# Smaller tiles for the in-chunk inverse of a gated delta rule: 32-token tiles on TensorE, two reductions moved off VectorE, and a new order

## What is computed

```python
q = l2norm(x @ Wq); k = l2norm(x @ Wk); v = x @ Wv      # per head
q, k, v = (silu(causal_conv4(t)) for t in (q, k, v))
beta = sigmoid(x @ Wb)
g = -exp(A_log) * softplus((x @ Wfa) @ Wfb + dt_bias)   # decay per channel
def step(S, (q, k, v, g, b)):                           # over the tokens
    S = S * exp(g)[..., :, None]
    err = v - einsum('bhk,bhkv->bhv', k, S)
    S = S + b * k[..., :, None] * err[..., None, :]
    return S, einsum('bhk,bhkv->bhv', q, S)
out = rmsnorm(attn) * rms_scale * sigmoid((x @ Wga) @ Wgb)
x = x + out @ Wo
```

## Time and profile before

| | |
|---|---|
| median of 3 runs | 1009.48 us (1007.05 to 1011.78) |
| the profiled execution, its own time | 1013.73 us |
| its span, first to last instruction | 1011.9 us |
| mean granted TensorE clock | 0.982 |
| TensorE busy | 949.9 us, 94% |
| VectorE busy | 812.7 us, 80% |
| ScalarE busy | 708.2 us, 70% |
| GpSimd busy | 73.9 us, 7% |

### The profile page before, as it was taken

How to read it: one execution, slowest core, us unless ns; L and a number is a source line. 1 busy time by engine, 2 the same in 40 slices (tenths; PEclk the granted TensorE clock), 3 DMA queues, 4 the chain that set the end, 5 groups by cost and what they waited for, 6 DMA issues and landing times.

```text
span 1011.9 us, 34566 instructions
## 1 busy us (share of the span) xinstructions
PE 949.9 (94%) x15274; PEld 721.6 (71%) x15274; DVE 812.7 (80%) x1707; ACT 708.2 (70%) x1556; POOL 73.9 (7%) x179
## 2 busy tenths in 40 slices
PE   4888699999999999999999999999999998999986
PEld 3534367777777777777777777777777777788774
DVE  5577679889888888889888898888888888777644
ACT  2376658887787778787778787877877787545441
POOL 7000000000000000000000000000000000000010
PEclk9898789999999999999999999999999999999999
DMA  6100010100000101200001000200000000000001
GB/s 164 49 1 13 29 31 31 41 13 13 13 3 2 31 31 31 72 13 13 13 2 29 21 17 28 82 13 3 13 13 13 13 13 13 13 13 3 3 2 42
DMA packets 29033, 24.14 MB, mean 24 GB/s; under 512 B 4626, under 2 KB 24276, under 8 KB 28884
## 3 DMA queue, kind: packets, MB, share of 16 engines
q1 hardware_dynamic: 28884, 21.94, 7.9%
HBM read 20.82 MB, written 1.11 MB: 22 GB/s over the span
## 4 chain that ended last, share of the span: by engine, by line
PE 87%; DVE 5%; ACT 4%; POOL 2%; issue 1%; POOLq 0%; DVEq 0%; ACTq 0%
PE psum L824 17%; PE psum L847 10%; PE psum L888 8%; PE psum L870 8%; PE psum L879 7%; PE psum L947 6%; PE psum L834 3%; PE psum L925 3%; PE psum L830 3%; PE psum L919 3%; PE psum L912 3%; PE psum L905 3%; PE psum L839 2%; PE psum L854 2%; PE psum L898 2%; PE psum L936 2%
## 5 line engine op out<-in xcount | busy, mean ns | idle before, releaser
L824 PE MATMUL psum<-hT,gw 128*128 128x512 f32 x384 | 189.9, 621 | 1.7 <-DVE pairs L1275 0.9
L847 PEld LDWEIGHTS psum<-kq,ks 128*64 128x64 f32 x3072 | 106.3, 139 | 74.8 <-issue 44.0
L1231 DVE SCALAR_TENSOR_TENSOR qkv<-pad,chan,qkv 128x512 f32<-128x512 f32 x192 | 135.7, 754 | 0.3
L847 PE MATMUL psum<-kq,ks 128*64 128x64 f32 x3072 | 124.0, 227 | 8.8 <-DVE tot L1269 4.5
L1257 DVE TENSOR_TENSOR kq<-kq,tot 128x512 f32<-128x512 f32 x160 | 110.3, 689 | 25.0 <-PE psum L847 25.0
L824 PEld LDWEIGHTS psum<-hT,gw 128*128 128x128 f32 x384 | 69.1, 197 | 64.3 <-issue 61.0
L1275 DVE COPY_PREDICATED pairs<-masks,psum 128x256 f32<-128x256 uint8 x192 | 102.1, 532 | 4.1 <-PE psum L847 4.1
L870 PE MATMUL psum<-tmat,pairs 64*64 64x32 f32 x2560 | 102.3, 220 | 2.9 <-ACT tmat L556 2.5
L870 PEld LDWEIGHTS psum<-tmat,pairs 64*64 64x64 f32 x2560 | 89.5, 135 | 18.9 <-issue 11.5
L888 PE MATMUL psum<-pairs,fmat 64*64 64x32 f32 x2560 | 101.8, 220 | 0.9 <-DVE fmat L1242 0.9
L888 PEld LDWEIGHTS psum<-pairs,fmat 64*64 64x64 f32 x2560 | 90.0, 136 | 9.1 <-issue 5.8
(11 more groups left out here) (163 smaller groups left out, 1695.0 us busy)
## 6 DMA issues: line engine op xcount, KB each, us to landing
bb<-beta_rows SPq DMA_DIRECT2D x32, 256.0 KB, 3.3
gw<-in_L_attn_Wq SPq DMA_DIRECT2D x16, 128.0 KB, 2.2
gw<-in_L_attn_Wk SPq DMA_DIRECT2D x16, 128.0 KB, 2.3
gw<-in_L_attn_Wv SPq DMA_DIRECT2D x16, 128.0 KB, 2.2
gwo<-in_L_attn_Wo SPq DMA_DIRECT2D x4, 512.0 KB, 5.8
x<-in_L_attn_hidden_states SPq DMA_DIRECT2D x4, 256.0 KB, 4.4
gfb<-in_L_attn_Wfb SPq DMA_DIRECT2D x16, 64.0 KB, 2.1
ggb<-in_L_attn_Wgb SPq DMA_DIRECT2D x4, 256.0 KB, 4.9
```

The costliest lines, as they stand in the source:

```text
L824: last = eng.matmul(two(bank[to]), gw[:, t, kt, hh * D:(hh + 1) * D], two(hT[:, kt])[:, :, h * PW:(h + 1) * PW], start=(kt == 0), stop=(kt ...
L847: last = eng.matmul(o[rows(b), :, u], ks[:, p, tokens(b, u)], half(kq[:, p, :, tokens(b, u)], h, 1), start=True, stop=True)
L1231: last = eng.scalar_tensor_tensor(out=piece(t, i), in0=src, scalar=tap_weight(t, tap, i), in1=piece(t, i), op0=ALU.mult, op1=ALU.add)
```

## The change

Four things are done at once.

1. **Tiles of 32 tokens.** Levels 0 to 4 never join a token of the first 32 of a cell with one of the last 32. So `level_products` (levels 0 to 4), `first_natural`, `inverse_y`, `inverse_natural` and `inverse_turned` (levels 1 to 4) issue, for each cell, two products of half the size on the diagonal blocks instead of one: 16 products (32 records), each with 32 stationary columns and a moving side half as wide. `inverse_y` and `inverse_turned` of level 5 keep 64 columns and contract over 32 tokens instead of 64. `diagonal` and level 5's products stay as they are. Since the off-diagonal blocks are no longer written, the banks are zeroed once at the start, and GpSimd clears a block of `tt` in each step.
2. **Output squares.** ScalarE squares in four instructions of 128x128 with `accum_out`, which give the sums; VectorE's `tensor_reduce` of 128x512 goes.
3. **Decay totals.** `tots[1]` (128x256) and `tots[2]` (128x128) are formed on GpSimd instead of VectorE.
4. **Order.** Every engine's `slot` is written in another order, with other PSUM banks and other waits. The silu of the keys and queries, the first decay and level 0 of a step stand one slot earlier on ScalarE and VectorE.

```diff
+QUARTER = P // 4
-L_BANK = (2, 0, 2, 0, 1, 0)
-Y_BANK = (None, 1, 3, 3, 3, 3)
+L_BANK = (7, 3, 0, 0, 6, 1)
+Y_BANK = (None, 3, 4, 1, 5, 4)
...
+        def block_of(ap, b, u, j):
+
+            return ap[quarter(b, j), u * C + j * QUARTER:u * C + (j + 1) * QUARTER]
...
+            def block_totals(p, l, first=None):
+                if l:
+                    lower, upper = totals(l)
+                    return eng.tensor_tensor(tots[l + 1], lower, upper, ALU.mult)
+                lower, upper = first_pairs(first)
+                return eng.tensor_tensor(tots[1].rearrange("p (m n) -> p m n", m=G * B), lower, upper, ALU.mult)
+
+            def clear_turned(p):
+                for b in range(B):
+                    last = eng.memset(tt[quarter(b, 1), p, :].rearrange("p (u i) -> p u i", i=C)[:, :, 0:QUARTER], 0.0)
+                return last
...
+            def square_output():
+                for u in range(G):
+                    last = eng.activation(unit(osq, u), unit(bank[O_BANK], u), ACT.Square, accum_out=ssq[:, 0, u:u + 1])
+                return last
...
-                    eng.activation(osq, bank[O_BANK][:, :], ACT.Square).then_inc(osq_ready, 1)
...
             def level_products(p, l):
                 h = LEVELS[l]
                 o = bank[L_BANK[l]][:, 0:UC].rearrange("p (a u n t) -> p a u n t", a=2, u=G, t=h)
+                if l == NL - 1:
+                    for u in range(G):
...
+                per = QUARTER // (2 * h)
                 for u in range(G):
                     for b in range(B):
-                        last = eng.matmul(o[rows(b), :, u], ks[:, p, tokens(b, u)],
-                                          half(kq[:, p, :, tokens(b, u)], h, 1), start=True, stop=True)
+                        for j in range(2):
+                            at = slice(u * P + b * C + j * QUARTER, u * P + b * C + (j + 1) * QUARTER)
+                            to = slice(b * C + j * QUARTER, b * C + (j + 1) * QUARTER)
+                            last = eng.matmul(o[to, :, u, j * per:(j + 1) * per], ks[:, p, at],
+                                              half(kq[:, p, :, at], h, 1), start=True, stop=True)
                 return last
...
+            def block_products(o, l, left, right, upper):
+                h = LEVELS[l]
+                per = QUARTER // (2 * h)
+                for u in range(G):
+                    for b in range(B):
+                        for j in range(2):
+                            last = eng.matmul(o[quarter(b, j), u, j * per:(j + 1) * per], block_of(left, b, u, j),
+                                              half(block_of(right, b, u, j), h, upper), start=True, stop=True)
+                return last
...
-                        last = eng.matmul(o[rows(b), u], cell(nmat[:, l], b, u), half(cell(tmat, b, u), h, 0),
-                                          start=True, stop=True)
+                        last = eng.matmul(o[rows(b), u], cell(nmat[:, l], b, u)[0:QUARTER], half(cell(tmat, b, u), h, 0)[0:QUARTER],
+                                          start=True, stop=True)
...
+            eng.memset(psum[:, :, 0:UC], 0.0)
...
-                eng.tensor_tensor(ks_l, ks_l, upper, ALU.mult)
-                return eng.tensor_tensor(tots[1].rearrange("p (m n) -> p m n", m=gb), lower, upper, ALU.mult)
+                return eng.tensor_tensor(ks_l, ks_l, upper, ALU.mult)
...
-                    eng.tensor_reduce(ssq[:, 0], gd(osq), AX.X, ALU.add).then_inc(ssq_ready, 1)
```

More of the change, by code:

```diff
@@ L876, in inverse_natural @@
                 o = bank[TM_BANK[l]][:, 0:HC].rearrange("p (u n t) -> p u n t", u=G, t=h)
-                for u in range(G):
-                    for b in range(B):
-                        last = eng.matmul(o[rows(b), u], cell(tt[:, p], b, u), half(cell(fmat[:, l - 1], b, u), h, 0),
-                                          start=True, stop=True)
-                return last
+                return block_products(o, l, tt[:, p], fmat[:, l - 1], 0)
             def inverse_turned(p, l):
@@ L1254, in decays @@
                 if l:
-                    lower, upper = (tots[l].rearrange("p (n t) -> p n t", t=2)[:, :, i] for i in range(2))
+                    lower, upper = totals(l)
                     nb = HU // h
@@ new lines, in slot @@
+                if 0 <= nm1 < NCK:
+                    after(kraw_ready, nm1 + 1)
+                    eng.wait_ge(in_beta[q], 16 * (nm1 // 2) + 16)
+                    eng.tensor_tensor(ks[:, q], kraw[:, 0], bb[:, q], ALU.mult).then_inc(kb_ready, 1)
+                if 0 <= n0 < NCK:
+                    after(level4_done, n0 + 1)
+                    decays(p, 4)
+                    after(y3_done, n0 + 1)
+                    inverse_sum(3).then_inc(summed3, 1)
+                    keep_pairs(p, 4).then_inc(kept4, 1)
@@ new lines, in slot @@
+                if 0 <= nm1 < NCK:
+                    after(level0_done, nm1 + 1)
+                    decays(q, 0, chunk(dec, nm1 % NCH))
+                if 0 <= n1 < NCK:
+                    after(osq_ready, n1 + 1)
+                    eng.scalar_tensor_tensor(out=og, in0=gate[:, n1 % 2], scalar=1.0, in1=bank[O_BANK][:, :], op0=ALU.add, op1=ALU.mult).then_inc(og_ready, 1)
+                if 0 <= nm1 < NCK:
+                    after(diag_ready, nm1 + 1)
+                    keep_pairs(q, 0).then_inc(kept0, 1)
@@ L1396, in _ @@
             ln_centre(2, 0)
-            for t in range(NCK - 2, NCK + 1):
+            for t in range(NCK - 2, NCK):
                 slot(t)
             ln_scale(2, 0)
+            slot(NCK)
+            ln_move(2, 0)
             slot(NCK + 1)
```

638 lines of the change are left out of this document (341 added, 297 removed).

## The result

The changed kernel takes **983.1 us** (median of 4 runs, 976.8 to 987.7) where the kernel before took 1010.6 beside it on the same chip. The ratio is 0.972, with an interval of 0.969 to 0.976: 2.8% faster, where 7.8% were forecast. The direction and the range hold, the likeliest value is 52 us too low. Medians here count every execution; the ratios leave out those over 1.5% above the fastest of the same kernel. The profiled execution of the changed kernel is the fastest of its four, 976.8 us.

A forecast was written before the change was run, and what follows sets the result against it. TensorE was taken to bound the kernel; a slot of 27.5 us less 3.8 plus 1.0 plus 0.3 of waits gave 25.0, saving 78 us in all, so 931 us, range 903 to 985.

The forecast's parts named there:

- What bounds the kernel: Full slots: TensorE has no idle time worth naming and sets the 27.5 us slot; VectorE is busy 24.0 us of it.
- Term 1: 18 small TensorE groups a slot: 32-column tiles, four at once, cut a group from 0.47 to 0.26 us, gaining 3.8 us.
- The rule of the Trainium skill: TensorE's small matmuls: starts never closer than about 25 ns, so a 32-record group costs 0.80 us and the kernel some 1230.
- Term 2: TensorE's changes of matmul shape: 14 a slot become 24, at 0.1 us each, a loss of 1.0 us per slot.
- Term 3: Moved work a slot: VectorE falls 1.4 to 22.6 us, ScalarE rises 0.9 to 22.4, GpSimd at most 3 more, hidden.
- Term 4: Waits between engines from the new order, tightest before level 1's `inverse_natural`: 0.3 us a slot, making the slot 25.0.
- Rival B: Full slots: TensorE's work shrinks as forecast but order waits are 1 to 2 us a slot; 965 to 1000 us, 20%.
- The sum: Whole kernel: 66 us from the full slots, 8 and 2 at the end, 2 in the first slot; 78 us saved.
- The tail's "2 us each": The four last slots, without projections: 2 us saved in each, 8 us, with 2 us more for the drain behind them.
- Ahead of the first slot: The kernel's start before the first slot: left as it is, no saving counted.
- Rival E: Small groups: the granted clock falls because less of the array works; stretches at 0.50 cost their work again; 3%.

The follow-up runs named there:

- squares_back: levels64 with the output's squares again one ScalarE pass and summed by a VectorE reduction; 978.3 us, ratio 0.966.
- order_only64: The changed kernel with 64-token products everywhere, keeping the new order, squares and totals; 1028.7 us, ratio 1.017.
- inverse64: The changed kernel with 64-token products in the inverse only, the levels staying in 32-token tiles; 1005.4 us, ratio 0.994.
- hybrid: The changed kernel with the level products of levels 0 and 2 back at 64 tokens; 972.5 us, ratio 0.963.
- levels64: The changed kernel with 64-token products in the levels only, the inverse staying in 32-token tiles; 976.8 us, ratio 0.966.
- hybrid3_fill: The changed kernel with levels 0, 2 and 4 at 64 tokens and four idle products in each of the four last full slots; 963.3 us, ratio 0.949.
- tiles_only: The kernel before, with its order, squares and totals, given only the 32-token tiles and their zeroing and clearing; 1044.8 us, ratio 1.030.
- loopfill_spread: The changed kernel with eight idle products a slot, four at each of two places among the small groups; 1062.4 us, ratio 1.049.

## Why the prediction was wrong

- **What bounds the kernel** was right: TensorE sets the slot before and after. squares_back shows that VectorE, on which I kept an eye, doesn't.
- **Term 1** was right in mechanism and size: 0.26 us said, 0.27 measured, four products at once. The rule of the Trainium skill, "TensorE: Matmul & The Clock Gate", in "Wait — 56ns, not 53.3ns?", does not hold for these tiles: 32 starts in 0.27 us are 8.4 ns apart on average, not 25. The 4 ns between different tiles of the same page of the Trainium skill, "Part 3: Packing small matmuls", is nearer.
- **Term 2** was right: 0.11 us a change; I counted 14 and 24, the traces show 13 and 23.
- TensorE's own work was thus forecast at 24.7, and with the waits at 25.0; the slot without a stop is 25.1 us, nearly all of it own work, so its own work was forecast 0.4 us too low and the waits too high.
- **Term 3** sized GpSimd right (a total of 128x256 takes 0.85 us) and it stayed hidden. Each accumulator read on ScalarE costs 0.22 us beside a square of 0.29, so 4 x 0.51 = 2.0 us a slot, above my 1.5 and my upper end of 1.9; it cost nothing.
- **Term 4**, the waits from the order, was 0.3 us a slot. In full slots I find hardly any (7.9 us over 28 slots behind the first start, nearly all in the first two and the last; before 8.8). Rival B's time came true, 983 in 965 to 1000, but its mechanism did not: that is chance.
- **The sum is where it failed.** "The stretch from 139 to 870 us holds 26.6 slots: 26.6 x 2.5 = 66 us" takes it that every slot runs at the pace of the array's work plus the waits for other engines. TensorE's own supply of instructions is missing in it. Over the first 28 slots the gain is 36 us; at 2.5 a slot it would have been 70. Of the 34 us missing, 18.7 are stops above 0.1 us, and the trace shows that the supply takes more than these. Twenty-two full slots have the same records. Set record by record against the fastest of them, 25.14 us, the others are 24.2 us longer in sum, and 22.4 of these us are lost at places 192 to 196 of a block of 256, some in delays too short to show as idle time. Of the rest, 3.5 us are 25.14 less the forecast's 24.98 in 22 slots, 4.5 fall on the three slots of a group's first chunk (3.0 in stops, some 1.6 in the half clock at 355.9), and 2 on the second slot. Less their stops, two of those three are 2.5 us shorter than before, as forecast.
- **The tail's "2 us each"** and 2 us of drain gave 10 us; it became 7 us longer (140.7 to 147.8 from the 29th slot's start). There are two causes side by side, 9.0 us of stops and, between 878 and 936 us, 23.9 us at half clock where there was none before. The clock fell behind or in waits of 1.8 us and more. The wait for VectorE belongs to the new order: order_only64 and inverse64, which have no stop at all, have it with 1.3 us, and their clock fell behind it once in four slots and three times in four. Idle work in that place gives 7.4 us back in hybrid and 6.6 in levels64 (the latter within the intervals); in the changed kernel it gave 0.7, and how the loss divides there stays open.
- Ahead of the first slot I had left all as it was; the new order begins 7.8 us earlier, which I had not foreseen. Without this luck the miss would be 60 us. The trace's saving of 36.8 us is these 7.8 and 36.2 in the 28 slots, less 7.2 behind them. The median lies 6.3 us above the profiled execution, and no trace shows those.
- **Rival E** gave the clock 3% on the ground that it held with idle time at the end. It fell in just that stretch, and once for 3.4 us in a full slot. Ahead of each of these falls stood an idle piece of TensorE and not only small groups, so E's reason did not hold.

What could have been seen beforehand: the trace of before has 120 transfers of 16 KB in its instruction queue for 2 x 15274 instructions, the closest 3.50 us apart. Four groups x32 behind one another have 64 instructions each, 256 in all, and by term 1 would be through in 4 x 0.26 = 1.0 us. That it would stop there, and not only draw on what had been brought ahead, these rows alone could not tell.

## What to carry to other kernels

Halving a product's size doubles its instructions; before counting the gain, find the shortest time in which the new program would issue 256, 512 and 1024 instructions, and compare it with one, two and four times the closest spacing of the instruction queue's transfers (13.2 us for four here). A single fast block does little harm: levels64 has 256 in 2.1 us and 5 stops. The densest 1024 of the full slots took 27.7 us before and 21.3 in inverse64 (no stop), 15.6 in levels64 (5 stops), 14.0 in the changed kernel (33), 12.1 in tiles_only (70); loopfill_spread, 16.2 and 17 stops, fits less well. Where that is too fast, leave part of the products whole and put wide ones between the small ones: hybrid3_fill, with two levels in tiles instead of five and idle work at the end, is 2.4% faster than the changed kernel. Idle time "<-issue" in the middle of a group, behind no semaphore, is the mark of it, and the proof is that such places lie whole multiples of 256 instructions apart.

## What the runs showed of the hardware

- TensorE's instructions are brought 256 at a time (16 KB), one transfer for each 256 issued (waits counted), and TensorE stops at the edge of such a block: all 416 stops of the traces stand at places 193 to 195 of one. In the changed kernel a transfer takes 0.9 to 1.5 us, the next starts 3.30 us after its start at the earliest (3.22 in any trace), and TensorE goes on 1.2 to 1.6 us after its end. Up to 1.9 us were lost at once in the changed kernel. Why one transfer started as late as 608.80, after 487 instructions, I don't know; weights were being loaded beside it.
- Four 32x32 tiles run at once for little more: 32 records in 0.27 us, 34 ns a round of four, where half of the 55 ns of 64 columns would be 28. A group of 16 in two 64-row halves took 0.44 to 0.49.
- The granted clock fell to 0.50 in the changed kernel's tail at 878.1, 902.0 and 925.9 us, behind or in idle pieces of TensorE of 1.8, 1.8 and 2.7 us, and at 355.9 us behind one of 1.9. It did not fall behind the stop of 1.68 us at 183.02. Before, it held at 1.00 in the tail, behind an idle piece of 1.96 us too. In tiles_only it fell 10 times in 25 full slots, where TensorE stopped once a slot or more.
